# A two-layer gated cross-attention kernel: last output weights in the query weights' buffers, and new orders at the transitions

## The chip, the cores and the metric

One NeuronCore of one Trainium2 chip runs the whole computation in one launch. The metric is the device time of that launch in microseconds (us). Five engines run side by side, each through its own queue of instructions in a fixed order: TensorE (PE in the profile), VectorE (DVE), ScalarE (ACT), GpSimd (POOL) and SyncE (SP, which here only issues DMA transfers). They meet through semaphores: an instruction waits until a count is reached, and whatever stands behind it in its queue waits too.

## The reference

x is 16 sequences of 64 tokens with 512 features, 1024 tokens in all. Four blocks are each added to x through a gate.

```python
x = x + tanh(g_xattn[0]) * attention0(layernorm(x), ctx, mask0, rotary positions)   # 32 query heads, 8 key heads, D = 128
x = x + tanh(g_ffn[0])   * experts(layernorm(x))       # 16 experts of 56, top 2: silu(x g) * (x u), weighted, then d
x = x + tanh(g_xattn[1]) * attention1(layernorm(x), ctx, mask1)                     # RMS norm of queries and keys, no rotation
x = x + tanh(g_ffn[1])   * lora(layernorm(x))          # 4 low-rank experts of rank 16, top 2, softmax gates
```

Attention is softmax(q k / sqrt(D)) v, then the output weights.

## The kernel before

Every fp32 product on TensorE is made of three: each operand is split into a high part (a rounded copy that ScalarE writes, names in _hi) and a low part (the difference, names in _lo, by VectorE or GpSimd), and `three` (L213 to L217) issues hi*hi, hi*lo and lo*hi. So each weight that is loaded (_raw) needs a pass of ScalarE and one of GpSimd before TensorE can use it.

The stages in order: keys and values of both layers (`kv_*`, eight blocks, the last of them, LATE, runs inside the first attention step), attention of layer 0 (`att_*`, lay = 0), the experts (`moe_*`), attention of layer 1 (lay = 1), the low-rank experts (`lora_*`).

Attention has 8 groups g of J = 4 heads, and each is done for two halves h of the tokens: a unit u = 2g + h, from 0 to 15. The work is a software pipeline. `step(g, h)` projects the queries of unit u, makes scores and softmax of u - 1, and values and output projection of u - 2. Per unit the chain is: scores (PE, L867), transposition (`turn_scores`, DVE), for layer 1 a scale by the norms (`scale_scores`, from `square_sums`, `turn_sums` and `norms`), mask, `maxima` (a reduction and four 32x32 operations, L1214), `att_shift`, `exponentials` (ACT), `sums` (again with four small operations, and a reciprocal), `att_normalise`, `turn_probs`, `probs_high` (ACT), `att_probs_low`, then `values` (PE, L888), `out_high` (ACT), `out_low` (DVE), `project_out` (PE, L215 to L217 into ps_b) and `add_output` (DVE). In layer 0 a query is also rotated: `rotate` on DVE reads the bank in three operations, `rotate` on POOL (L1094) adds the two halves.

The order of every engine's queue is written out by hand, in one `step` for each engine (`att_act`, `att_pool`, `att_dve`, `att_pe`, `att_sync`). Steps at the ends have orders of their own: `first_scores` (layer 0, g = 0, h = 1), `second_first_scores` (the same in layer 1), `before_closing` (g = 7, h = 1), and what stands behind the loop, here called the closing: units 14 and 15 with nothing left to project. The first steps, to (1, 0), are called the opening.

In the closing the splits of the next stage's weights run beside: `beside(h, t)` calls `moe_beside_act` (ACT's high parts, by the table SPLITS) or `lora_beside_*`. The list `splits` counts router r, gate g, up u and down d pieces from 0 to 21, and GpSimd makes the low parts in the same order (`moe_pool`). The output weights of group g are split by `wo_high` (L977) and `wo_low` (L1087), those of the last group behind the last step, into the same wo_hi and wo_lo as all others. `ln_stat`, `ln_sd`, `ln_rs`, `ln_norm`, `ln_turn`, `ln_high` and `ln_low` are the steps of the layer norm. `tokens` in `moe_*` copies the normalised tokens of one tile to f_hi and f_lo, from which `up` reads.

On SP the spill of the LATE block stands ahead of the first loads of layer 0:

```python
kv_sync_spill(sp, LATE)                            # 8 transfers of 512 KB
sp.wait_ge(kv["v_spilled"], 16 * 2 * GB * 2 * NB)
...
load_wo(0)
load_v(0)
```

## Time and profile before

| | us |
|---|---|
| median of three runs | 1278.47 (1278.26 to 1282.9) |
| the profiled execution | 1278.5 |
| its span, first to last instruction | 1276.5 |
| TensorE busy | 1208.3 |
| mean granted clock of TensorE, share of full | 0.982 |

PE, PEld, DVE, ACT, POOL and SP are the engines; L977 is line 977 of the kernel. A timeline line gives the start and length in us, the engine, the line, the operation, output and inputs, shape and count, and in brackets how long the engine stood idle before it and which instruction released it. The busy share is an average over stages; an engine that is idle beside a busy TensorE costs nothing.

### The profile page before, as it was taken

What the parts mean: (1) busy time and instruction counts of PE and PEld (TensorE: products, weight loads), DVE (VectorE), ACT (ScalarE), POOL (GpSimd) and SP (SyncE); (2) the same over time, 40 slices, a digit from 0 to 9 for tenths busy, and PEclk for the clock granted to TensorE, in tenths of its full rate; (3) what the DMA queues carried; (4) which work ended last, traced back from release to release, by engine and by line L of the source; (5) the groups of instructions that cost most, each with busy time, mean ns of one, the idle gap of its engine ahead of it and who ended that gap; (6) DMA issues with size and microseconds to landing.
All of it is one profiled execution on the core that took longest, in us unless ns stands there. A gap on an engine that the chain in (4) does not pass through costs nothing.

```text
span 1276.5 us, 16865 instructions
## 1 busy us (share of the span) xinstructions
PE 1208.3 (95%) x6160; PEld 956.9 (75%) x6160; DVE 852.1 (67%) x1477; ACT 428.4 (34%) x732; POOL 581.9 (46%) x399
## 2 busy tenths in 40 slices
PE   7999999799999999999799999799999999999976
PEld 6887878587777877777588887577777777777664
DVE  4656635988888878888953125857666666757586
ACT  5144151222222222222353225444334344443422
POOL 4431432556767667574443112345455464544400
PEclk9999999899999999999799999999999999999997
DMA  7853730922212122212010003202122112211001
GB/s 264 265 149 123 240 118 22 301 79 74 74 53 101 43 74 74 82 42 99 1 59 33 1 0 130 82 9 101 48 74 74 49 66 82 74 41 42 33 1 67
DMA packets 57248, 106.73 MB, mean 84 GB/s; under 512 B 3504, under 2 KB 36272, under 8 KB 51824
## 3 DMA queue, kind: packets, MB, share of 16 engines
q1 hardware_dynamic: 56672, 105.04, 24.0%
q0 software_dynamic: 384, 1.05, 0.2%
q8 instruction: 30, 0.49, 0.2%
q14 instruction: 18, 0.15, 0.0%
q10 hardware_dynamic: 144, 0.00, 0.0%
HBM read 78.81 MB, written 27.26 MB: 83 GB/s over the span
## 4 chain that ended last, share of the span: by engine, by line
PE 67%; DVE 14%; POOL 8%; issue 6%; ACT 3%; DMA 1%; SPq 1%; POOLq 0%; ACTq 0%; DVEq 0%
PE ps_b L215 11%; PE ps_b L217 11%; PE ps_b L216 11%; PE ps_q L215 9%; PE ps_q L216 9%; PE ps_q L217 9%; DVE r_s L1198 2%; PE ps_s L867 2%; PE ps_b L888 2%; POOL qT L1094 2%; POOL wo_lo L1087 2%; PE ps_q L854 1%; DVE o_lo L1241 1%; POOL wq_lo L682 1%; DVE mx_c L1214 1%
## 5 line engine op out<-in xcount | busy, mean ns | idle before, releaser
L215 PE MATMUL ps_b<-wo_hi,o_hi 128*128 128x512 f32 x512 | 203.7, 398 | 12.9 <-DVE o_lo L1241 4.1
L215 PE MATMUL ps_q<-hT_hi,wq_hi 128*128 128x512 f32 x512 | 207.5, 405 | 5.7 <-ACT qT L986 4.4
L217 PE MATMUL ps_b<-wo_hi,o_lo 128*128 128x512 f32 x512 | 202.0, 394 | 0.0
L216 PE MATMUL ps_b<-wo_lo,o_hi 128*128 128x512 f32 x512 | 201.9, 394 | 0.0
L216 PE MATMUL ps_q<-hT_lo,wq_hi 128*128 128x512 f32 x512 | 200.3, 391 | 0.0
L217 PE MATMUL ps_q<-hT_hi,wq_lo 128*128 128x512 f32 x512 | 199.8, 390 | 0.0
L1241 DVE TENSOR_TENSOR o_lo<-ps_b,o_hi 128x512 fp32r<-128x512 f32 x128 | 82.4, 685 | 77.2 <-ACT o_hi L1011 75.8
L1250 DVE SCALAR_TENSOR_TENSOR x_sb<-ps_b,gates,x_sb 128x512 f32<-128x512 f32 x128 | 92.3, 727 | 61.4 <-PE ps_b L217 60.9
L1094 POOL TENSOR_TENSOR qT<-q_t 128x512 f32<-128x512 f32 x64 | 88.8, 1387 | 96.3 <-DVE q_t L1178 96.3
L215 PEld LDWEIGHTS ps_q<-hT_hi,wq_hi 128*128 128x128 f32 x512 | 96.3, 188 | 42.6 <-issue 15.2
L215 PEld LDWEIGHTS ps_b<-wo_hi,o_hi 128*128 128x128 f32 x512 | 97.9, 191 | 38.2 <-issue 13.8
L682 POOL TENSOR_TENSOR wq_lo<-wq_raw,wq_hi 128x512 fp32r<-128x512 f32 x64 | 89.5, 1403 | 55.1 <-ACT wq_hi L676 55.1
L217 PEld LDWEIGHTS ps_b<-wo_hi,o_lo 128*128 128x128 f32 x512 | 97.7, 191 | 20.9
L216 PEld LDWEIGHTS ps_b<-wo_lo,o_hi 128*128 128x128 f32 x512 | 97.8, 191 | 20.0
L217 PEld LDWEIGHTS ps_q<-hT_hi,wq_lo 128*128 128x128 f32 x512 | 96.4, 188 | 21.0
L216 PEld LDWEIGHTS ps_q<-hT_lo,wq_hi 128*128 128x128 f32 x512 | 96.5, 188 | 17.8
L1006 ACT ACTIVATE p_hi<-pT 128x1024 fp32r<-128x1024 f32 x32 | 33.9, 1060 | 204.1 <-DVE pT L1235 204.1
L1087 POOL TENSOR_TENSOR wo_lo<-wo_raw,wo_hi 128x512 fp32r<-128x512 f32 x64 | 85.7, 1356 | 28.7 <-ACT wo_hi L977 28.7
L735 POOL TENSOR_TENSOR p_lo<-pT,p_hi 128x1024 fp32r<-128x1024 f32 x27 | 64.2, 2380 | 63.1 <-ACT p_hi L1006 63.1
L1011 ACT ACTIVATE o_hi<-ps_b 128x512 fp32r<-128x512 f32 x128 | 66.4, 607 | 66.5 <-PE ps_b L888 66.4
L724 POOL TENSOR_TENSOR s_sb<-s_sb,mx_c 128x1024 f32<-128x1024 f32 x28 | 53.7, 1918 | 70.7 <-DVE mx_c L1214 70.7
L730 POOL TENSOR_TENSOR p_sb<-p_sb,p_rec 128x1024 f32<-128x1024 f32 x28 | 53.7, 1919 | 65.6 <-DVE p_rec L1229 65.6
(236 smaller groups left out, 2395.5 us busy)
## 6 DMA issues: line engine op xcount, KB each, us to landing
wq_raw<-in_wq SPq DMA_DIRECT2D x16, 1024.0 KB, 4.8
wo_raw<-in_wo SPq DMA_DIRECT2D x16, 1024.0 KB, 4.9
v_hi_spill<-vs_hi SPq DMA_DIRECT2D x16, 512.0 KB, 5.7
v_lo_spill<-vs_lo SPq DMA_DIRECT2D x16, 512.0 KB, 6.7
kT<-kT_spill SPq DMA_DIRECT2D x32, 256.0 KB, 4.3
v_hi<-v_hi_spill SPq DMA_DIRECT2D x16, 512.0 KB, 3.7
v_lo<-v_lo_spill SPq DMA_DIRECT2D x16, 512.0 KB, 4.6
kw_raw<-in_wk SPq DMA_DIRECT2D x4, 1024.0 KB, 8.9
```

Source lines behind the costliest of these rows:

```text
L215: nc.tensor.matmul(dst, l_hi, r_hi, start=first, stop=False)
L216: nc.tensor.matmul(dst, l_hi, r_lo, start=False, stop=False)
L217: return nc.tensor.matmul(dst, l_lo, r_hi, start=False, stop=last)
L682: nc.gpsimd.tensor_tensor(wq_lo[:, :, j * D:(j + 1) * D], wq_raw[:, :, j * D:(j + 1) * D], wq_hi[:, :, j * D:(j + 1) * D].bitcast(F32), AL ...
L724: eng.tensor_tensor(sc, sc, wide(mx_c[:, :], QB), ALU.subtract).then_inc(c["s_shifted"], 1)
L730: eng.tensor_tensor(pr, pr, wide(p_rec[:, :], QB), ALU.mult).then_inc(c["p_normed"], 1)
L735: eng.tensor_tensor(p_lo[:, :], pT[:, :], p_hi[:, :].bitcast(F32), ALU.subtract).then_inc(c["p_lo"], 1)
L1011: nc.scalar.activation(o_hi[:, 2 * half:2 * half + 2, :, par * S:(par + 1) * S], ps_b[n].rearrange("p (t j q) -> p t j q", t=2, j=J), ACT. ...
L1087: nc.gpsimd.tensor_tensor(wo_lo[:, j, :], wo_raw[:, j, :], wo_hi[:, j, :].bitcast(F32), ALU.subtract).then_inc(c["wo_lo"], 1)
L1094: nc.gpsimd.tensor_tensor(qT[:, h, j, :], q_t1[:, j % 2, :], q_t2[:, j % 2, :], ALU.add).then_inc(c["q_rot"], 1)
L1241: nc.vector.tensor_tensor(o_lo[part], ps_b[n].rearrange("p (t j q) -> p t j q", t=2, j=J), o_hi[part].bitcast(F32), ALU.subtract).then_inc ...
L1250: nc.vector.scalar_tensor_tensor(x_sb[:, i, :], ps_b[t][:, :], gates[:, lay:lay + 1], x_sb[:, i, :], ALU.mult, ALU.add).then_inc(c["y_adde ...
```

## The change

In words:

- The output weights of the last group go into wq_hi and wq_lo (`wo_parts`), whose last reader is the last query projection. So `wo_high` and `wo_low` of that group move into the step ahead of the closing, in both layers. `before_closing` holds for layer 1 too.
- GpSimd waits at the end of attention for the last p_lo; the expert splits come behind it, in the order r, g0 to g3, u0 to u3, g4 to g6, u4 to u6, d, and `up` waits for the pieces of its half. u_raw and d_raw lie elsewhere, the u load waits for the output projections of 14 units, the d load for all.
- The first three tiles of `up` read hT_hi and hT_lo directly, without `tokens`.
- Opening of layer 0: the LATE values are spilled in three parts (24 transfers), `load_v(0)` goes ahead of the last part, `load_wo(0)` behind it; shift and normalisation of unit 0 go from DVE to POOL; the maxima come ahead of the last value tile, and one more rotation is taken ahead.
- Opening of layer 1: `wo_high(0)` and `wo_low(0)` go one step earlier, the fourth query ahead of the exponential, and the next unit's `turn_sums` ahead of `sums`.
- Last closing: the mask goes from POOL to DVE, aT_lo and the clears from DVE to POOL, bT_lo to a later place; the order of layer 0 holds for both. The square root and reciprocal of the last layer norm become Ln and Exp on ScalarE.

```diff
...
-                                                    ("rT_lo", [P, KC, P], FR), ("gu1", [P, 2, FH], F32))
-        with ExitStack() as a:
-            d_raw, = alloc(a, ("d_raw", [P, FT, E], F32))
+            r_raw, rT_hi, rT_lo, gu1, d_raw = alloc(a, ("r_raw", [P, KC, P], F32), ("rT_hi", [P, KC, P], FR), ("rT_lo", [P, KC, P], FR),
+                                                    ("gu1", [P, 2, FH], F32), ("d_raw", [P, FT, E], F32))
...
 
+        with ExitStack() as a:
...
 
+        def ln_rs_act(act, c, h, parts=HALVES):
+            act.wait_ge(*c("moments", parts[h][1]))
+            own = slice(*parts[h])
+            nc.scalar.activation(ln_sd_sb[:, own], ln_mv[:, own, 1], ACT.Ln, bias=eps_ln[:, 0:1]).then_inc(c["sd"], 1)
+            act.wait_ge(*c("sd", h + 1))
...
+            v = VALUE_BLOCKS.index(LATE)
+            i0, i1 = part
+            sp.wait_ge(c["v_hi"], NT * v + i1)
+            sp.wait_ge(c["v_lo"], NT * v + i1)
+            for st, dr in ((vs_hi, v_hi_dram), (vs_lo, v_lo_dram)):
+                for g in range(GB):
+                    sp.dma_start(dr[lay, cb * GB + g, :, i0 * D:i1 * D].rearrange("p (i d) -> p i d", d=D),
+                                 st[:, i0:i1, g * D:(g + 1) * D].bitcast(F32)).then_inc(c["v_late"], 16)
...
-            return lay == 0 and isinstance(g, int) and (g, h) == (G - 1, 1)
+            return isinstance(g, int) and (g, h) == (G - 1, 1)
...
-                kv_sync_spill(sp, LATE)
-                sp.wait_ge(kv["v_spilled"], 16 * 2 * GB * 2 * NB)
+                kv_sync_late(sp, LATE_PARTS[0])
+                kv_sync_late(sp, LATE_PARTS[1])
+                sp.wait_ge(kv["v_spilled"], 16 * 2 * GB * LATE_VALUES)
+                sp.wait_ge(kv["tile"], NT * len(BLOCKS))
+                load_v(0)
+                kv_sync_late(sp, LATE_PARTS[2])
+                sp.wait_ge(kv["v_late"], LATE_SPILLS)
...
-            load_v(0)
...
+            return (wq_hi, wq_lo) if isinstance(g, int) and g == G - 1 else (wo_hi, wo_lo)
...
+                if isinstance(g, int) and g == G - 1:
+                    act.wait_ge(*c("q_done", J * 2 * G))
+                elif not (isinstance(g, int) and g == 0):
                     act.wait_ge(*c("y_done", 8 * g))
...
-                    if second_first_scores(lay, g, h):
-                        wo_high(0, j)
...
-                    if second_first_scores(lay, g, h) and j == 3:
-                        exponentials(us)
                     if do_project and lay:
-                        queries(uq, h, j)
+                        if not (isinstance(g, int) and (g, h, j) == (1, 0, 0)):
+                            queries(uq, h, j)
+                        if isinstance(g, int) and (g, h) == (0, 0):
+                            wo_high(0, j)
...
-                if do_score and not second_first_scores(lay, g, h):
+                if before_closing(lay, g, h):
+                    for j in range(J):
+                        wo_high(G - 1, j)
+                if do_score:
                     exponentials(us)
                 if next_wq:
                     att_wq_high(act, lay, g + 1, 3)
+                if first_scores(lay, g, h):
+                    wo_high(0, 0)
+                    wo_high(0, 1)
+                if second_first_scores(lay, g, h):
+                    queries(uq + 1, 0, 0)
                 if do_score:
                     probs_high(us)
                 if last_step(lay, g, h):
                     norms(us + 1)
                 if first_scores(lay, g, h):
-                    for j in range(J):
-                        wo_high(0, j)
+                    wo_high(0, 2)
+                    wo_high(0, 3)
...
-            for j in range(J):
-                wo_high(G - 1, j)
-            if lay:
-                beside(0, -1)
             for n in range(4):
                 out_high(last - 1, n)
-            if lay == 0:
-                beside(0, -1)
+            beside(0, -1)
             exponentials(last)
-            beside(0, 0)
             probs_high(last)
             if lay == 0:
                 nc.scalar.preload_act_table_set("sqrt_and_others")
             for n in range(4):
                 out_high(last, n)
-            ln_sd(act, lns[2 * lay + 1], 0)
+            beside(1, -1)
+            if lay:
+                ln_rs_act(act, lns[3], 0)
+            else:
+                ln_sd(act, lns[1], 0)
...
+                    att_shift(pool, lay, us)
                     split((), (0,))
                     added(2)
+                    added(3)
                     split((), (1,))
-                    added(3)
+                    att_normalise(pool, lay, us)
                     split((), (2, 3))
                     return
                 if second_first_scores(lay, g, h):
                     for j in range(J):
+                        att_wq_low(pool, lay, 1, j)
+                    return
+                if lay and isinstance(g, int) and (g, h) == (0, 0):
+                    for j in range(J):
                         wo_low(0, j)
-                        att_wq_low(pool, lay, 1, j)
                     return
...
                     att_shift(pool, lay, us)
+                if before_closing(lay, g, h):
+                    wo_low(G - 1, 0)
+                    wo_low(G - 1, 1)
                 added(3)
+                if before_closing(lay, g, h):
+                    wo_low(G - 1, 2)
...
             att_steps(pool, step)
-            for j in range(J):
-                wo_low(G - 1, j)
+            pool.wait_ge(*c("p_lo", 2 * G))
             if lay:
...
                     rotated(0)
                     rotated(1)
                     turn_scores(us, 1 - h)
+                    maxima(us)
                     kv_values_lo(dve, LATE, NT - 1)
                     rotated(2)
-                    maxima(us)
                     rotated(3)
-                    att_shift(dve, lay, us)
+                    sums(us)
                     rotate(uq + 1, 0, 0)
-                    sums(us)
-                    att_normalise(dve, lay, us)
                     turn_probs(us)
+                    rotate(uq + 1, 0, 1)
                     att_probs_low(dve, lay, us)
...
                         scale_scores(us)
...
+                att_mask(dve, lay, last, 1)
...
-            if lay:
-                out_low(last - 1, 2)
-                out_low(last - 1, 3)
             att_shift(dve, lay, last)
-            if lay:
-                add_output(last - 1, 0, 0)
...
+            out_low(last - 1, 2)
+            out_low(last - 1, 3)
+            sums(last)
+            att_normalise(dve, lay, last)
+            add_output(last - 1, 0, 0)
+            turn_probs(last)
+            for t in range(1, PAIRS):
+                add_output(last - 1, 0, t)
+            att_probs_low(dve, lay, last)
+            ln_stat(dve, ln, 0, added)
+            ln_stat(dve, ln, 1, added)
...
-            ln_rs(dve, ln, 0)
+            if lay == 0:
+                ln_rs(dve, ln, 0)
...
             sp.wait_ge(c["w_hi"], len(splits))
             sp.wait_ge(c["w_lo"], len(splits))
             sp.wait_ge(c["logits"], 2)
+            sp.wait_ge(c["hid"], 4)
             att_load_wq(sp, 1, 0)
 
 
 
-        splits = [("r", 0)] + [(w, n) for w in "gud" for n in range(FT)]
-        SPLITS = {(0, -1): (0, 1, 2, 3, 4, 5), (0, 0): (6, 7), (1, 0): (8,), (1, 1): (9, 10), (1, 2): (11, 12), (1, 3): (13, 14)}
+        splits = ([("r", 0)] + [(w, n) for w in "gu" for n in range(4)] + [(w, n) for w in "gu" for n in range(4, FT)]
+                  + [("d", n) for n in range(FT)])
+        GU_SPLITS = {("g", 0): 5, ("u", 0): 9, ("g", 1): 12, ("u", 1): 15}
...
 
@@ -1482,14 +1522,19 @@
 
             def up(i, r, half, between=None):
 
-                if half == 0:
-                    pe.wait_ge(c["f_hi"], i + 1)
-                    pe.wait_ge(c["f_lo"], i + 1)
+                direct = isinstance(i, int) and i < 3
+                if half == 0 and not direct:
+                    pe.wait_ge(c["f_hi"], i - 2)
+                    pe.wait_ge(c["f_lo"], i - 2)
                 if not (isinstance(i, int) and i == 0):
                     pe.wait_ge(c["gu"], 2 * i + half - 1)
                 for bank, hi, lo, name in ((ps_q[half], gT_hi, gT_lo, "g_done"), (ps_b[half], uT_hi, uT_lo, "u_done")):
+                    if isinstance(i, int) and i == 0:
+                        pe.wait_ge(c["w_lo"], GU_SPLITS[name[0], half])
                     for k in range(KC):
-                        last = three(bank[:, 0:FH], f_hi[:, r, k, :], f_lo[:, r, k, :], hi[:, k, half * FH:(half + 1) * FH],
...
             pe.wait_ge(*att[0]("y_added", 2 * G * PAIRS))
-            pe.wait_ge(c["w_lo"], 1 + 2 * FT)
...
@@ -1600,11 +1644,9 @@
                 hidden_hi(i - 1)
                 silu(i, 1)
 
-            act.wait_ge(c["w_lo"], 1 + FT)
-            tokens(0, 0)
             ln_sd(act, lns[1], 1)
             logits(0)
-            tokens(1, 1)
+            act.wait_ge(c["w_lo"], GU_SPLITS["g", 1])
             silu(0, 0)
...
@@ -1670,13 +1711,9 @@
                 weigh(i, 1)
 
             pool.wait_ge(*lns[1]("lo", PAIRS))
-            pool.wait_ge(c["w_lo"], 1 + FT)
-            tokens(0, 0)
-            tokens(1, 1)
+            pool.wait_ge(c["w_lo"], GU_SPLITS["g", 1])
             for n in range(FT):
                 split_low(pool, 1 + 2 * FT + n)
-                if n == 1:
-                    tokens(2, 0)
             pool.wait_ge(c["x_w"], 1)
...
-                ln_sd(nc.scalar, lns[3], 1, PARTS)
+                ln_rs_act(nc.scalar, lns[3], 1, PARTS)
...
+            if (h, t) == (1, 1):
                 nc.vector.wait_ge(lora["w_hi"], 2)
                 nc.vector.scalar_tensor_tensor(bT_lo[:, :], b_raw[:, :], LORA_SCALE, bT_hi[:, :].bitcast(F32), ALU.mult,
                                                ALU.subtract).then_inc(lora["w_lo"], 1)
+
+        def lora_pool(pool):
+            pool.wait_ge(*att[1]("q_done", J * 2 * G))
...
             ln_norm(dve, lns[3], NT - 2)
-            ln_rs(dve, lns[3], 2, PARTS)
...
```

## Rows read from the trace of the kernel before

**Rows 1.** Page: busy time and share of each engine; 40 slices
```profile
PE 1208.3 (95%) x6160; PEld 956.9 (75%) x6160; DVE 852.1 (67%) x1477; ACT 428.4 (34%) x732; POOL 581.9 (46%) x399
...
PE   7999999799999999999799999799999999999976
...
PEclk9999999899999999999799999999999999999997
```

**Rows 2.** Waits of TensorE: total us, times, longest us
```profile
PE ps_q L854 <- ACT q_sq L985: 5.2, 2, 4.5
PE ps_b L888 <- DVE x_sb L1250: 4.7, 1, 4.7
...
PE ps_s L867 <- POOL qT L1094: 4.4, 1, 4.4
PE ps_b L888 <- DMA v_lo<-v_lo_spill: 3.6, 1, 3.6
```

**Rows 3.** Timelines, opening of layer 0: start us, length us, what, idle before
```profile
234.34 2.27 PE L867 MATMUL ps_s<-qT,kT 128*64 128x256 f32 x10 [4.40 <-POOL qT L1094]
...
253.62 0.47 PE L215 MATMUL ps_b<-wo_hi,o_hi 128*128 128x512 f32 x1 [0.20 <-POOL wo_lo L1087]
...
231.98 2.31 POOL L1094 TENSOR_TENSOR qT<-q_t 128x512 f32<-128x512 f32 x1 [2.69 <-DVE q_t L1178]
...
242.47 1.23 DVE L735 TENSOR_TENSOR p_lo<-pT,p_hi 128x1024 fp32r<-128x1024 f32 x1 [1.12 <-ACT p_hi L1006]
...
227.52 7.24 SPq L407 DMA_DIRECT2D v_lo_spill<-vs_lo  x4
239.59 0.34 SPq L741 DMA_DIRECT2D wo_raw<-in_wo  x1
...
240.45 0.43 SPq L748 DMA_DIRECT2D v_lo<-v_lo_spill  x1
```

**Rows 4.** Windows of 2 us, TensorE: stretch, length, busy, clock, DMA, GB/s
```profile
608.00:610.00 2.00, 0.00 (x0) 1.00 0.00 0
610.00:612.00 2.00, 1.89 (x5) 0.50 0.00 0
...
614.00:616.00 2.00, 2.00 (x10) 1.00 0.00 0
```

**Rows 5.** Timelines, closing of layer 0
```profile
592.49 0.77 DVE L1214 TENSOR_TENSOR mx_c<-mx_a 32x32 f32<-32x32 f32 x4
...
606.54 2.28 DVE L718 TENSOR_TENSOR s_sb<-s_sb,mask_i 128x1024 f32<-128x1024 f32 x1
...
611.18 5.03 DVE L1214 TENSOR_TENSOR mx_c<-mx_a 32x32 f32<-32x32 f32 x4
616.24 2.25 DVE L724 TENSOR_TENSOR s_sb<-s_sb,mx_c 128x1024 f32<-128x1024 f32 x1
...
619.71 1.22 DVE L1225 TENSOR_REDUCE sm_a<-p_sb 128x32 f32<-128x1024 f32 x1
...
612.39 7.23 POOL L1449 TENSOR_TENSOR gT_lo<-g_raw,gT_hi 128x512 fp32r<-128x512 f32 x5
...
629.88 0.39 PE L888 MATMUL ps_b<-p_hi,v_hi 64*128 64x256 f32 x2 [2.73 <-DVE p_lo L735]
```

**Rows 6.** Timelines, opening of the expert layer
```profile
644.77 7.53 POOL L1449 TENSOR_TENSOR uT_lo<-u_raw,uT_hi 128x512 fp32r<-128x512 f32 x6 [3.28 <-ACT uT_hi L1444]
...
653.28 0.44 PE L215 MATMUL ps_q<-gT_hi,f_hi 128*128 128x448 f32 x1 [1.56 <-POOL f_lo L1655]
...
647.11 0.70 DVE L223 BATCH_NORM_STATS2 ln_stats<-x_sb 128x6 f32<-128x512 f32 x1
```

**Rows 7.** Timelines, opening of layer 1
```profile
818.37 1.93 PE L854 MATMUL ps_q<-q_sq,ones 128*32 128x512 f32 x8 [4.52 <-ACT q_sq L985]
...
816.68 1.15 ACT L999 ACTIVATE p_sb<-s_sb,zero_b 128x1024 f32<-128x1024 f32 x1 [3.30 <-DVE s_sb L724]
...
809.48 4.92 DVE L1214 TENSOR_TENSOR mx_c<-mx_a 32x32 f32<-32x32 f32 x4
...
825.05 1.23 DVE L735 TENSOR_TENSOR p_lo<-pT,p_hi 128x1024 fp32r<-128x1024 f32 x1 [1.13 <-ACT p_hi L1006]
```

**Rows 8.** Timelines, closing of layer 1
```profile
1206.09 5.97 POOL L1087 TENSOR_TENSOR wo_lo<-wo_raw,wo_hi 128x512 fp32r<-128x512 f32 x4
1212.03 2.37 POOL L718 TENSOR_TENSOR s_sb<-s_sb,mask_sb 128x1024 f32<-128x1024 f32 x1
...
1228.31 0.58 PE L888 MATMUL ps_b<-p_hi,v_hi 64*128 64x256 f32 x2 [4.67 <-DVE x_sb L1250]
```

88 lines of the change are left out of this document (38 added, 50 removed).

## The prediction

> **What bounds the kernel now.** I read the busy shares and the 40 slices first. TensorE is busy 95% of the span, and the clock row is at 9 (its top digit) but for one 8 and two 7s, in slices where the work changes kind [rows 1]. Inside the long attention loops there is nothing to win: TensorE is full, and the other engines have room. Everything lies in some 68 us where TensorE isn't busy (1276.5 less 1208.3), and in the stretches where its clock is low because it had just waited. TensorE's list of waits names the places [rows 2]: 5.2 us for squares from ScalarE, 4.7 for an added output, 4.4 for a rotated query, 3.6 for the values' load. By their times they belong to the four transitions of attention: the two openings (about 225 to 254 and 788 to 838) and the two closings (605 to 653 and 1203 to 1236). The kernel's first 20 us and its last 25 us also have gaps, and the change leaves nearly all of those alone.
>
> **The clock.** After the 2.97 us gap ahead of 610.12 the granted clock is 0.50, that is 1.2 GHz, and from 614 it is 1.00 (2.4 GHz) again [rows 4]. 24 matmuls take 7.3 us there and 5.6 us at full clock, so a gap that long costs 1.7 us more than its own length. A gap that shrinks enough gives that back too; a gap that only moves doesn't.
>
> **Opening of layer 0.** Now TensorE stands 4.40 us until 234.34, for the rotated query that GpSimd makes at 231.98 with a stretched 2.31 us [rows 3]. It is late because VectorE takes the score maxima ahead of the last rotation. Then it stands 3.6 us for the values, queued on SP behind eight spills of 512 KB (the last four issue over 7.24 us) and the output weights. After: the spill goes in parts as tiles are ready, and values load right after the last tile. GpSimd takes shift and normalisation, VectorE has them no more and reaches the last rotation some 2.5 us sooner; score(1) can start near 230.6, a gain of 3.7, plus 1.6 of clock, since the gap left is under 1 us. From there I walk each queue with the durations of before. VectorE: sums and rotation to 234.9, transposition of probabilities to 236.2, the second rotation to 238.3, low halves of probabilities to 239.5, or 240.6 if GpSimd's output-weight splits hold it up; values(0) start there and not at 247.2. But what comes next is late: the fourth wo_lo stands in GpSimd's queue behind the third query's addition, and that waits for VectorE's mask and rotation (about 246). So wo_lo ends near 248.6 and the first output projection starts at 248.7, against 253.62 now [rows 3]. That is 4.9 us, less 1.7, since the new 4 us gap ahead of it brings a low clock: **-3.3**. The load of the output weights now waits for the last small spills. I cost those at 0.4 us an issue (the values' issues on the same queue take 0.43): 224.5 to 228, landed by 231, weights there by 236 and their splits just ahead of p_hi, which ScalarE's order puts behind two of them. By the nearest spill rows, 7.24/4 = 1.81 us each, it would be 14.5 us for eight, and the weights would land near 250 and hold p_hi up: +5. Ends: -6 to +5. I take the small price because each piece is an eighth of the size of those in [rows 3].
>
> **Rule against it.** The Trainium skill (DMA: Bandwidth & Descriptors, Measured) says that transfers under 64 KB are dominated by descriptors and wants 1 MiB; the change cuts 8 transfers into 24, the last eight of 64 KB. By its 0.95 us for 64 KB the last eight would be an estimated 7.6 us and the weights about 4 us later than I say, so that the term would be 0 to +1.
>
> **Closing of layer 0.** The chain is VectorE's. While GpSimd works without a pause through wo_lo, router and gate splits (five of them in 7.23 us), four 32x32 maxima take 5.03 us; ten microseconds earlier, with GpSimd idle, the same four take 0.77 [rows 5]. The shift takes 2.25 for 1.23, the mask 2.28 for 1.23, the sums 2.27 for 0.77: together 7.8 us over. The change sets these splits aside until after the last p_lo, and makes the four wo_lo a step earlier, in the query weights' buffers, whose last reader ends at 592.4. Not free: they now stand ahead of the normalisation in GpSimd's queue, and the four small sums of that step (0.77 us at 598.56) will be held up three times. Normalisation ends near 604.5 and not 601.7, the low halves at 608.2 and not 605.35, so values(14) start **2.75 us later**. From 608.2: transposition, mask, two low outputs, maxima, shift, two low outputs, exponential, sums, normalisation come to 620.3; probabilities turned by 622.3. Now TensorE is late next: its four projections start at 612.2, take 11.2 us at full clock, 12.2 with half a low stretch, and the last addition and p_lo follow: 626.4. Values(15) start at 629.88 now [rows 5]: **-3.5**, ends -6 (clock up, chain of VectorE alone) and 0 (clock low through both pairs).
>
> **Opening of the expert layer.** TensorE waits 1.56 us for f_lo until 653.28, after the last of the u splits [rows 6]. The change reads hT directly and waits only for the splits of its half: -1.56. Against it: the splits now run from p_lo on, beside the layer norm, so that the first two normalisations (SBUF to SBUF, 0.50 each) each wait up to 1.3 us, and ln_sd stands behind four u_hi (2.5 us, covered by the first projection at low clock, 4.9 us now). **-1.3**, ends -1.6 and 0. The u load moves to the end of projection 13 (603) and needs some 8 to 10 us; its first reader is at 629. The d load is covered as well.
>
> **Opening of layer 1.** TensorE stands 4.52 us until 818.37 for q_sq, which is queued on ScalarE behind the exponential (816.68, itself waiting for VectorE's shift, whose four maxima took 4.92 us beside GpSimd) [rows 7]. After: squares come first, the wo splits are in the step before. That step pays 0.7 us (two ln_high later by 0.6, a normalisation beside wo_lo). Then: TensorE free at 814.6, squares at 815.2, sums and score to 818.2, projections to 820.9, 823.7, 826.5. VectorE blocks on turn_sums until 816.3, then copies (some held up by the last wq_lo) to 819.6, sums to 821.9, normalisation, transposition, and p_lo to 826.9, against 826.28 now [rows 7]. So values(0) start at 827.0 instead of 833.20, and nothing of 1.27, 0.26 and the low clock is left. The fourth projection ends at 831.4 and o_lo is there: **-6.3** against 837.67. Ends -7.5 and -4: p_lo has 0.5 us to spare at most, and each microsecond it is late costs one.
>
> **Closing of layer 1.** Here the four wo_lo (5.97 us) hold the mask on GpSimd until 1214.40 [rows 8]. After: wo_lo a step earlier, mask and p_lo on VectorE. The price is as in layer 0: the exponential 0.9 later, sums and normalisation 2.1 later, values(14) at 1207.1 for 1206.23. Scale, mask and low outputs then run to 1212.2; TensorE starts its projections there and not at 1209.76, after a 3.4 us gap, so at low clock: 1225.1 for the fourth, p_lo 1227.1, values(15) at 1227.15 for 1228.31. **-1.5** with 0.3 for a shorter stay at the low clock; ends -4.5 (no low clock) and +1.5. Ln and Exp on ScalarE for a square root and VectorE's reciprocal put some 0.15 us on each of two late steps: **+0.3**, ends 0 and +0.6.
>
> **Sum.** -3.3 - 3.5 - 1.3 - 6.3 - 1.5 + 0.3 = -15.6. The profiled execution took 1278.5 (span 1276.5 and 2.0 around it), the median of three is 1278.47: 1262.9.
>
> **Rivals.**
> - *Only the openings pay* (0.17). In both closings the 2.75 and 0.9 us at the front and the clock eat the rest. For: the chain there hops engines at each step, and TensorE's last projections are next in line. Against: 7.8 us of hold-ups go. 1278.5 - 3.3 - 1.3 - 6.3 + 0.3 = 1267.9.
> - *The clock stays up* (0.14). If the gaps that are left no longer pull it down in three of the stretches I costed low, 3 x 1.7 more: 1257.8. For: a gap of 1.27 in the opening of layer 1 didn't. Against: the one of 2.46 ahead of 619.84 did.
> - *The late spill isn't cheaper* (0.07), that is, the opening of layer 0 doesn't become what the change says: +5 for -3.3: 1271.2. It decides once the output weights land after about 237.
> - *GpSimd's splits hold up the layer norm* (0.05), the slower case. All fifteen expert splits now run between p_lo(15) and the end of the router's product. If each held up one instruction on VectorE's chain, 15 x 1.26 = 18.9: 1281.8. Against: bn_stats took 0.70 us amid six u splits (7.53 us) [rows 6], and so did PSUM readers; only the normalisations were stretched. It becomes slower from about twelve holds on. The Trainium skill (SBUF — State Buffer, Who interferes with whom) has the same rule: an instruction with two SBUF inputs, or tensor_scalar in a two-port mode, is fully blocked by GpSimd, tensor_reduce and a single SBUF input are not. The trace agrees (sm_a 1.22 us beside a split, 1.22 alone).
> - The rest, 0.57, is the forecast.
>
> **How the numbers follow.** The likeliest case gives 1263. The range 1254 to 1271 takes in the clock case and the openings-only case and most of the terms' ends, which don't all fall together. A change of 0.5% is 6.4 us, about what a measurement of this kernel can tell from none. Below 1272.1: forecast, openings only, clock, and a part of the spill case, 0.90; above 1284.9: 0.03, the far end of the split case; between: 0.07.
>
> **What would show it.** Right: no wait for q_sq near 814 and values(0) of layer 1 about 13 us after it; mx_c x4 near 0.8 us in both closings, and sm_c of the step before at 2.5 or more; up(0) right behind the router's product; p_lo of layer 0 near 240, with a wait for wo_lo after it. Wrong: wo_raw landing after 237, the first projection of layer 0 after 250, values(15) of the closings no earlier than now, a layer norm longer than now by over 2 us.

## Result and profile after

The changed kernel takes **1263.32 us** (median of 4 runs, 1261.83 to 1264.48), the kernel before, beside it, 1279.14 us. The ratio is 0.9872, 95% interval 0.9852 to 0.9893. The forecast was 1263. The profiled execution took 1262.69 us, of which 1260.7 are its span.

The page of the changed kernel, busy time and slices:

```profile
PE 1204.3 (96%) x6160; PEld 955.8 (76%) x6160; DVE 840.5 (67%) x1471; ACT 425.3 (34%) x730; POOL 577.9 (46%) x399
...
PEclk9999999999999999999899999999999999999987
```

Against [rows 1], TensorE does the same 6160 matmuls with 4.0 us less of busy time (part of it is the clock: 0.984 on average for 0.982), and of the digits 8 and 7 in mid span only one is left. VectorE is busy 11.6 us less: part of that are its hold-ups by GpSimd, part is work that changed engines. TensorE's list of waits (total us, times, longest) shows what took the places of [rows 2]:

```profile
PE ps_b L921 <- DVE p_lo L759: 8.7, 4, 2.7
...
PE ps_b L215 <- POOL wo_lo L1125: 6.4, 7, 3.7
```

The four waits of 4.7 to 3.6 us are gone from the list: square sums and rotated query wait 0.69 and 0.64 us at most. In their place are four shorter waits for low halves of probabilities (2.71, 2.02, 1.93 and 2.02 us), one of 3.25 us ahead of the projections in the closing of layer 1, and one new one of 3.70 us, which is the one that the prediction names: the fourth wo_lo of the opening of layer 0. The opening of layer 0, timelines of the changed kernel (start us, length us, what, idle before):

```profile
223.60 1.80 SPq L430 DMA_DIRECT2D v_hi_spill<-vs_hi  x4
225.44 1.85 SPq L430 DMA_DIRECT2D v_lo_spill<-vs_lo  x4
229.06 0.33 SPq L765 DMA_DIRECT2D wo_raw<-in_wo  x1
...
233.86 1.15 ACT L1009 ACTIVATE wo_hi<-wo_raw 128x512 fp32r<-128x512 f32 x2 [6.91 <-DMA wo_raw<-in_wo]
...
229.80 1.51 PE L900 MATMUL ps_s<-qT,kT 128*64 128x256 f32 x12 [0.64 <-POOL qT L1132]
...
238.76 0.39 PE L921 MATMUL ps_b<-p_hi,v_hi 64*128 64x256 f32 x2 [0.60 <-issue]
...
247.11 0.77 PE L215 MATMUL ps_b<-wo_hi,o_hi 128*128 128x512 f32 x1 [3.70 <-POOL wo_lo L1125]
```

The last eight pieces take 3.65 us on SP's queue, 0.45 us each, where [rows 3] has 1.81. Score(1) starts at 229.80 for 234.34, values(0) at 238.76 for 247.23, the first projection at 247.11 for 253.62. Then the clock, in windows of 2 us (stretch, length, busy of PE, PEld, DVE, ACT and POOL, clock, DMA share, GB/s):

```profile
249.00:251.00 2.00, 2.00 (x6) 1.63 (x5) 1.90 (x3) 1.15 (x1) 0.59 (x1) 0.50 1.04 434
...
253.00:255.00 2.00, 2.00 (x10) 1.64 (x10) 1.94 (x5) 0.00 (x0) 0.00 (x0) 0.98 0.00 0
```

Behind the 3.70 us wait TensorE runs at 1.2 GHz until some 253; the 48 matmuls of the first projection take 2.8 us longer than in the kernel before (the first of the next group starts 13.78 us after 247.11, and 10.98 us after 253.62 before).

The closing of layer 0, VectorE and TensorE:

```profile
594.81 3.19 DVE L1262 TENSOR_TENSOR sm_c<-sm_a 32x32 f32<-32x32 f32 x4
...
608.80 0.77 DVE L1262 TENSOR_TENSOR mx_c<-mx_a 32x32 f32<-32x32 f32 x4
609.61 1.23 DVE L748 TENSOR_TENSOR s_sb<-s_sb,mx_c 128x1024 f32<-128x1024 f32 x1
...
604.12 0.39 PE L921 MATMUL ps_b<-p_hi,v_hi 64*128 64x256 f32 x2 [2.71 <-DVE p_lo L759]
...
622.64 0.39 PE L921 MATMUL ps_b<-p_hi,v_hi 64*128 64x256 f32 x2 [2.02 <-DVE p_lo L759]
```

The maxima, 5.03 us in [rows 5], take 0.77, the shift 1.23 for 2.25. The price is in the first line: the sums of the step before take 3.19 us for 0.77. In the opening of the expert layer, up(0) starts at 643.44 right behind the router's product, without the wait of 1.56 us of [rows 6]. The opening of layer 1:

```profile
806.71 1.06 PE L887 MATMUL ps_q<-q_sq,ones 128*32 128x512 f32 x8 [0.69 <-ACT q_sq L1017]
818.52 0.39 PE L921 MATMUL ps_b<-p_hi,v_hi 64*128 64x256 f32 x2 [0.49 <-issue]
...
800.88 0.77 DVE L1262 TENSOR_TENSOR mx_c<-mx_a 32x32 f32<-32x32 f32 x4
```

0.69 us of waiting where [rows 7] has 4.52, and values(0) 11.8 us after it.

### The profile page after: what moved, and what is told of

Same layout as the page of the kernel before. It is cut to its first block, busy times and chain, and to the rows that moved or that the text cites. A ratio compares the mean times of both kernels' runs of the same rounds, so it can differ in the third digit from the quotient of the medians.

```text
span 1260.7 us, 16869 instructions
## 1 busy us (share of the span) xinstructions
PE 1204.3 (96%) x6160; PEld 955.8 (76%) x6160; DVE 840.5 (67%) x1471; ACT 425.3 (34%) x730; POOL 577.9 (46%) x399
## 4 chain that ended last, share of the span: by engine, by line
PE 72%; DVE 11%; POOL 7%; issue 6%; ACT 3%; DMA 0%; POOLq 0%; ACTq 0%; DVEq 0%
PE ps_b L215 12%; PE ps_b L217 12%; PE ps_b L216 12%; PE ps_q L215 10%; PE ps_q L216 9%; PE ps_q L217 9%; PE ps_s L900 3%; PE ps_b L921 3%; DVE r_s L1246 2%; POOL qT L1132 2%; POOL wo_lo L1125 2%; POOL wq_lo L706 1%; PE ps_q L887 1%; POOL p_sb L754 1%; DVE o_lo L1289 1%
## 5 line engine op out<-in xcount | busy, mean ns | idle before, releaser
L215 PE MATMUL ps_b<-wo_hi,o_hi 128*128 128x512 f32 x448 | 176.2, 393 | 6.4 <-POOL wo_lo L1125 6.4
L216 PE MATMUL ps_b<-wo_lo,o_hi 128*128 128x512 f32 x448 | 175.5, 392 | 0.0
L217 PE MATMUL ps_b<-wo_hi,o_lo 128*128 128x512 f32 x448 | 175.3, 391 | 0.0
L215 PEld LDWEIGHTS ps_b<-wo_hi,o_hi 128*128 128x128 f32 x448 | 84.8, 189 | 27.5 <-issue 10.0
L217 PEld LDWEIGHTS ps_b<-wo_hi,o_lo 128*128 128x128 f32 x448 | 84.8, 189 | 17.8
L216 PEld LDWEIGHTS ps_b<-wo_lo,o_hi 128*128 128x128 f32 x448 | 84.8, 189 | 17.5
L1125 POOL TENSOR_TENSOR wo_lo<-wo_raw,wo_hi 128x512 fp32r<-128x512 f32 x56 | 73.5, 1327 | 13.2 <-ACT wo_hi L1009 13.2
```

Source lines behind the costliest of these rows:

```text
L215: nc.tensor.matmul(dst, l_hi, r_hi, start=first, stop=False)
L216: nc.tensor.matmul(dst, l_hi, r_lo, start=False, stop=False)
L217: return nc.tensor.matmul(dst, l_lo, r_hi, start=False, stop=last)
L1125: nc.gpsimd.tensor_tensor(lo[:, j, :], wo_raw[:, j, :], hi[:, j, :].bitcast(F32), ALU.subtract).then_inc(c["wo_lo"], 1)
```

## Experiments

All are edits of one of the two kernels. Ratios are to the kernel before, timed on the same chip beside them; where I give a difference to the changed kernel "by the ratios", it is the difference of two ratios times the kernel before. In the traces I compare distances between two instructions of the same execution, so that a gain elsewhere doesn't mix in. S(n), V(n) are score(n) and values(n).

**1. The opening of layer 1 alone.** The kernel before with the new order of layer 1's opening: squares and wo splits a step earlier, the exponential in its place of the step, the sums of rows turned behind it, wo_lo on GpSimd in the first step.

```
 ACT  second step of layer 1
-    wo_high(0, j)           # now in the first step
-    if j == 3: exponentials(us)
     queries(uq, h, j)
 ...
+exponentials(us)
 ...
+queries(uq + 1, 0, 0)       # first query of the next step
```

> The kernel before with the new opening of layer 1 alone (wo splits of group 0 one step earlier, fourth query ahead of the exponential, turn_sums of the next unit ahead of the sums). Theory: the transitions are independent terms, and this one is worth 6.3 us by itself: values(0) of layer 1 start 6.3 us sooner after the last expert product, and the time is 6.3 us (0.5%) under the kernel before. Rival: the stretch was only short because the stages ahead of it had moved too; then it gives under 3 us.

Measured: 1272.1 us (1269.85 to 1273.14), ratio 0.9951 (0.9937 to 0.9964). From the first square sums of layer 1 to the first out projection it is 31.03 us, as in the changed kernel (37.87 before). The other transitions take what they took before, to 0.1 us; what differs is the time before the late tile (0.9 us less) and behind values(15) of layer 1 (2.1 us more, with more of it at the low clock), where this edit changes nothing. TensorE in this kernel:

```profile
813.96 1.07 PE L854 MATMUL ps_q<-q_sq,ones 128*32 128x512 f32 x8 [0.69 <-ACT q_sq L985]
825.78 0.39 PE L888 MATMUL ps_b<-p_hi,v_hi 64*128 64x256 f32 x2 [0.49 <-issue]
```

From the last expert product to values(0) it is 6.36 us less than before. So this part alone is worth what its term says (-6.3), and it doesn't need the others.

**2. Which of the moves in that opening counts.** The changed kernel with the exponential ahead of the fourth query's squares again.

```
 for j in range(J):
+    if second_first_scores(lay, g, h) and j == 3:
+        exponentials(us)
     queries(uq, h, j)
 ...
-if do_score:
+if do_score and not second_first_scores(lay, g, h):
     exponentials(us)
```

> The changed kernel, but in the opening of layer 1 ScalarE takes the exponential ahead of the fourth query again, as before the change. Theory: the 4.52 us came from the late shift (four maxima held up for 4.92 us by GpSimd's splits), not from the place of the exponential; with the splits gone the shift ends at 802.9, before the fourth query is projected at 806.0, so this costs nothing: the wait ahead of the square sums stays 0.7 us and the time within 0.5 us of the changed kernel. Rival: the place in ScalarE's queue is the cause; then 2 to 4.5 us of the wait come back.

Measured: 1259.84 us, ratio 0.9853 (0.9838 to 0.9868), 2.4 us under the changed kernel by the ratios, with intervals that overlap. The wait ahead of the square sums is the same 0.69 us:

```profile
808.53 1.07 PE L887 MATMUL ps_q<-q_sq,ones 128*32 128x512 f32 x8 [0.69 <-ACT q_sq L1017]
```

What had held the squares up was the late exponential (VectorE's maxima amid GpSimd's splits), and the splits in ScalarE's queue, not the order of exponential and squares; how much each of the two counts isn't separated. This order is even 0.55 us better to the first out projection (30.48).

**3. The hold of the expert splits.** The changed kernel without GpSimd's wait for the last p_lo in layer 0, so that the splits run during the closing as they did before.

```
-pool.wait_ge(*c("p_lo", 2 * G))
 if lay:
+    pool.wait_ge(*c("p_lo", 2 * G))
     lora_pool(pool)
```

> The changed kernel, but GpSimd doesn't wait for the last p_lo in layer 0, so that router and first gate splits run beside the chain of VectorE again. Theory (GpSimd blocks VectorE's instructions with two SBUF inputs): mx_c x4 in the closing goes from 0.77 to about 5 us, p_lo(15) comes 3 to 4 us later (1.8 us of VectorE's slack before it are used up first), and the time is 2 to 4.5 us above the changed kernel. Rival: the closing is bound by TensorE's projections and hand-overs between engines; then values(15) start within 1 us of the changed kernel's.

Measured: 1265.39 us, ratio 0.9908 (0.9893 to 0.9923). VectorE and GpSimd:

```profile
608.37 4.48 DVE L1262 TENSOR_TENSOR mx_c<-mx_a 32x32 f32<-32x32 f32 x4
612.89 2.25 DVE L748 TENSOR_TENSOR s_sb<-s_sb,mx_c 128x1024 f32<-128x1024 f32 x1
...
609.03 5.02 POOL L1489 TENSOR_TENSOR gT_lo<-g_raw,gT_hi 128x512 fp32r<-128x512 f32 x4
```

The hold-up is back with the splits, same place, same instructions: 4.48 us for 0.77. From S(15) to V(15) it is 25.98 us, with the splits held 23.18 and 21.45 in the two profiled executions of the changed kernel. By the ratios the kernel is 4.6 us above the changed one, at the upper end of what I expected (its one profiled execution, 1262.96 us, is no longer than the changed kernel's, since the clock stayed up in two later places). The mechanism of the term for this closing is shown. The Trainium skill (SBUF — State Buffer, Who interferes with whom) has a VectorE instruction with two SBUF inputs wait for a GpSimd instruction that reads SBUF and was issued first. This pair of traces agrees and adds that one of 32x32 is hit as hard as one of 128x1024: the four lose 3.71 us, 0.93 each, the shift loses 1.02, and one split lasts 1.26.

**4. The old order of SP's queue.** The changed kernel with the whole late spill, and the values behind the output weights, as before.

```
-kv_sync_late(sp, LATE_PARTS[0])
-kv_sync_late(sp, LATE_PARTS[1])
-...
-load_v(0)
-kv_sync_late(sp, LATE_PARTS[2])
+kv_sync_spill(sp, LATE)
 load_wo(0)
+load_v(0)
```

> The changed kernel with the old order on SyncE: the whole late spill after the last tile, then output weights, then values. All other orders stay. Theory: the three-part spill carries the opening of layer 0: with the old one wo_raw lands near 243.5 and not 233.8, p_hi waits behind two wo_high, values(0) start about 8 us later, the first projection of the output 4 to 6 us later, and the time is 4 to 6 us above the changed kernel. Rival: the orders of VectorE and GpSimd carry it (the last rotation 3 us sooner); then the time is within 2 us of the changed kernel.

Measured: 1271.07 us, ratio 0.9952 (0.9937 to 0.9968): 10.2 us over the changed kernel by the ratios, twice what I had expected.

```profile
227.56 7.25 SPq L415 DMA_DIRECT2D v_lo_spill<-vs_lo  x4
239.65 0.34 SPq L765 DMA_DIRECT2D wo_raw<-in_wo  x1
...
248.97 0.58 PE L916 MATMUL ps_b<-p_hi,v_hi 64*128 64x256 f32 x2 [11.17 <-DVE p_lo L759]
```

The gap grows to 11.17 us, since in the new order of ScalarE the high half of the probabilities stands behind two wo_hi, and they wait for the weights. From the last matmul of the late tile to the first projection it is 37.1 us; 26.7 in the changed kernel, 32.2 before. Of these 10.4 us the group of 48 behind it gives some back, since it runs at full clock here (10.98 us, for 13.78 and 12.58 in the changed kernel): 7.6 to 8.8 us are left in the trace, and the rest of the 10.2 isn't placed. **Without the new spill the rest of this opening would lose 5 us.** It isn't a sum of two gains: one edit makes the other possible. Experiments 9 and 10 part the two halves of the spill's change.

**5. wo_lo ahead of the additions.** The prediction put the late fourth wo_lo down to its place in GpSimd's queue, behind an addition. Here the four wo_lo stand together, and VectorE makes the third rotation ahead of the maxima and behind the low outputs.

```
 added(0)
-wo_low(0, 0)
-wo_low(0, 1)
+for j in range(J): wo_low(0, j)
 added(1)
-wo_low(0, 2)
 added(2)
-wo_low(0, 3)
```

> The changed kernel with two moves in the opening of layer 0: GpSimd makes all four low parts of the first output weights ahead of the second rotated query, and VectorE takes the first two low outputs ahead of the third rotation. Theory (what is late next there is the fourth wo_lo, which stands behind a rotation in two queues): the 3.70 us wait ahead of the first output projection falls to 1 to 1.7 us, TensorE's clock then stays up and gives back some 2.8 us more, and the time is 4 to 5 us under the changed kernel. Rival: the wait only moves, to the low outputs or to values(1); then under 2 us.

Measured: 1258.34 us (1252.03 to 1261.39), ratio 0.9836 (0.9811 to 0.9860), beside 0.9866 for the changed kernel on the same chip (8, below): 3.8 us by the ratios and 2.7 by the medians, with intervals that overlap; I had given 4 to 5. The trace is clearer. GpSimd, then TensorE:

```profile
239.06 6.98 POOL L1125 TENSOR_TENSOR wo_lo<-wo_raw,wo_hi 128x512 fp32r<-128x512 f32 x4
...
246.18 0.47 PE L215 MATMUL ps_b<-wo_hi,o_hi 128*128 128x512 f32 x1 [1.25 <-POOL wo_lo L1125]
```

The wait is 1.25 us for 3.71, the projection starts 24.27 us after the late tile for 26.71, and the clock stays up: the windows over 246 to 254 read 1.00, and the group of 48 takes 10.99 us, where the changed kernel took 13.78 and 12.58. That is 2.4 plus 1.6 to 2.8: 4.0 to 5.2 us in the trace.

**6. Two wo splits on either side of the normalisation.** In the steps before both closings, GpSimd makes two of the wo_lo behind the normalisation, to take away the price that the first lines of the closing show (3.19 us of sums).

```
-if before_closing(lay, g, h):
-    wo_low(G - 1, 2)
-    wo_low(G - 1, 3)
 split((), (2,))
 if do_score:
     att_normalise(pool, lay, us)
+if before_closing(lay, g, h):
+    wo_low(G - 1, 2)
+    wo_low(G - 1, 3)
```

> The changed kernel, but in the step ahead of both closings GpSimd makes two of the four wo_lo ahead of the normalisation and two behind it. Theory (three of the four small sums wait for GpSimd's splits): sm_c x4 goes from 3.2 us to about 1.3 in layer 0 and from 2.2 to about 1 in layer 1, and values(14) start 1.5 to 2 us sooner in layer 0 and 1 us sooner in layer 1; since values(15) hang on the same chain, the time falls by 1.5 to 3 us. Rival: values(15) are bound by TensorE's four projections after values(14) and its clock; then what is won ahead is lost there and the time stays within 1 us.

Measured: 1260.84 us, ratio 0.9873 (0.9858 to 0.9888): no difference that can be measured from the changed kernel (0.9866), and none of the 1.5 to 3 us that my theory gave. In layer 0 the edit does what it should:

```profile
593.89 1.10 DVE L1262 TENSOR_TENSOR sm_c<-sm_a 32x32 f32<-32x32 f32 x4
...
601.10 0.39 PE L921 MATMUL ps_b<-p_hi,v_hi 64*128 64x256 f32 x2 [0.62 <-issue]
604.72 0.47 PE L215 MATMUL ps_b<-wq_hi,o_hi 128*128 128x512 f32 x1 [1.92 <-ACT o_hi L1043]
```

V(14) start 2.56 us after S(15) for 4.66, and the wait of 2.71 is gone; but the gap before the projections is 1.92 now and the clock goes down behind it (0.79 in 605 to 613), so that S(15) to V(15) is 20.96 us, for 23.18 and 21.45 in the two profiled executions of the changed kernel. In layer 1 it loses 0.7 us. The sums there are down to 0.77 us, but the moved splits now lie beside the copies of the row sums, 4.09 us for 2.07:

```profile
1178.99 0.77 DVE L1262 TENSOR_TENSOR sm_c<-sm_a 32x32 f32<-32x32 f32 x4
...
1181.48 4.09 DVE L1246 COPY r_s<-r_t 32x16 f32<-32x16 f32 x8
...
1182.10 2.53 POOL L1125 TENSOR_TENSOR wq_lo<-wo_raw,wq_hi 128x512 fp32r<-128x512 f32 x2
```

I had left that neighbour out. My theory held in layer 0 for values(14) and fell in layer 1. The time is where the rival put it (within 1 us), and the low clock that it named was seen, but with intervals of some 2 us on either side the times don't decide it.

**7. All three moves** (2, 5 and 6) in one kernel.

> The two kernels before this one together, and the exponential first in layer 1 (0.5 us sooner in its trace). Theory: the terms add up, 6 to 8.5 us under the changed kernel, about 1254 to 1256, ratio to the kernel before about 0.981. Rival: the gains overlap in a clock that falls by chance in the closings, and less than 4 us are left.

Measured: **1254.62 us** (1251.49 to 1256.99, 5 runs), ratio 0.9818 (0.9800 to 0.9837), the fastest of all: 1.8% under the kernel before, and 6.5 us under the changed kernel, with intervals that don't overlap: what I expected (6 to 8.5), and not the rival's under 4. Windows of this kernel over the closing of layer 0:

```profile
602.00:610.00 8.00, 8.00 (x36) 6.58 (x36) 7.72 (x17) 2.45 (x4) 0.00 (x0) 1.00 0.00 0
```

The same gap of 1.9 us ahead of the projections as in 6, and here the clock stays at 2.4 GHz. Left as it was in layer 1, where it loses 0.7 us, the move of 6 might leave this kernel a little faster still; that wasn't tried.

**8. The changed kernel again**, on the chip of 5 to 7.

> The changed kernel once more, beside the others. Theory: 15 to 17 us under the kernel before. The stretch from the last expert product to the first query of layer 1 took 4.9 us in some traces and 6.5 us in others, behind the same wait of 1.94 us and the same instructions, by whether the clock fell; both lengths are expected again over the four traces of this call.

Measured: 1261.08 us (1258.32 to 1262.73), ratio 0.9866 (0.9849 to 0.9884). Its windows behind the same wait of 3.71 us:

```profile
249.00:251.00 2.00, 2.00 (x7) 1.58 (x6) 1.97 (x4) 0.05 (x1) 1.92 (x1) 0.58 0.74 213
...
253.00:255.00 2.00, 2.00 (x11) 1.64 (x10) 1.92 (x3) 0.00 (x0) 0.65 (x1) 1.00 0.19 68
```

The same gap costs 1.6 us of clock here and 2.8 in the first execution: how long TensorE stays at 1.2 GHz isn't settled by the gap. The second half of what I had expected missed: both lengths of the stretch at the end of the expert layer were to be seen in the four traces of 5 to 8, and all four show the long one, with the low clock.

**9. The values last, the pieces kept.**

```
-load_v(0)
 kv_sync_late(sp, LATE_PARTS[2])
 sp.wait_ge(kv["v_late"], LATE_SPILLS)
+load_v(0)
```

> The changed kernel, but in the opening of layer 0 SP loads the first values behind the small late spills and their landing, ahead of the output weights, and no longer ahead of the last eight pieces; the pieces stay. It separates the two halves of the change to SP's queue: cutting the spills, and moving the values. Mine (the pieces carry it): the two value loads took 0.8 us on the queue, the small spills are issued about 1.3 us sooner, the values are issued near 227.5 instead of 221 and land by 233, the output weights are issued some 0.9 us later (their wait for the pieces counts from 226), and nobody reads the values before 238.8: values(0) and the first output projection start within 0.7 us of the changed kernel's, and the time is that of the changed kernel, ratio 0.985 to 0.989. Rival (the early values carry it): the values land behind the weights and hold up values(0) as in the kernel before, 3 us or more, ratio 0.990 or more.

Measured: 1263.38 us, ratio 0.9885 (0.9863 to 0.9907). By the ratio it is my case, but by the trace neither theory's: V(0) starts 2.7 us later after S(1), not under 0.7.

```profile
229.18 0.32 SPq L771 DMA_DIRECT2D v_hi<-v_hi_spill  x1
...
230.01 0.43 SPq L765 DMA_DIRECT2D wo_raw<-in_wo  x1
...
237.31 1.15 ACT L1009 ACTIVATE wo_hi<-wo_raw 128x512 fp32r<-128x512 f32 x2 [10.15 <-DMA wo_raw<-in_wo]
...
241.70 0.39 PE L921 MATMUL ps_b<-p_hi,v_hi 64*128 64x256 f32 x2 [3.37 <-issue]
```

The weights are issued 0.95 us later than in the changed kernel, as I had said, but the first wo_hi starts 7.30 us after the issue instead of 4.80: 1 MB of values is on its way just ahead of 1 MB of weights, and that is what this edit changes on the queue. What is late is the load behind them: ScalarE's high half of the probabilities stands behind two wo_hi, and V(0) behind it. Loading them early is worth 2.5 us to the first projection (26.7 for some 29.2), through the weights.

**10. The spill whole, the values ahead of it.**

```
-LATE_PARTS = ((0, 4), (4, NT - 1), (NT - 1, NT))
+LATE_PARTS = ((0, NT),)
...
 load_v(0)
-kv_sync_late(sp, LATE_PARTS[2])
+kv_sync_late(sp, LATE_PARTS[0])
```

> The changed kernel, but the late value block is spilled in eight issues of 512 KB, all after the last tile, as in the kernel before, and only the values' load ahead of them, as in the changed kernel. Mine (the pieces carry it): the values are there early, but the eight issues still take some 11.5 us from about 222 and the output weights wait some 4.8 us more for the landing: weights issued near 239, fourth high half near 245, and ScalarE's high half of the probabilities, which stands behind two of them, near 246; values(0) near 249 and the time that of the kernel with the old order throughout, ratio 0.994 to 0.997. Rival (the early values carry it): values(0) start near 239 to 241 and the ratio is 0.989 or less. The large step of that earlier kernel, 10.2 us where I had given 4 to 6, would be explained by mine: the wait for the weights on ScalarE delays values(0) by 10.2 us (238.76 to 248.97).

Measured: 1270.39 us, ratio 0.9931 (0.9915 to 0.9948). SP and TensorE:

```profile
226.19 4.24 SPq L430 DMA_DIRECT2D v_hi_spill<-vs_hi  x4
230.47 7.19 SPq L430 DMA_DIRECT2D v_lo_spill<-vs_lo  x4
242.59 0.34 SPq L765 DMA_DIRECT2D wo_raw<-in_wo  x1
...
251.75 0.58 PE L919 MATMUL ps_b<-p_hi,v_hi 64*128 64x256 f32 x2 [11.06 <-issue]
```

With the values in time, V(0) still start 19.4 us after S(1), as in experiment 4 (19.5), for 9.0 in the changed kernel. The ratio is a little under the 0.994 to 0.997 that I had given. The pieces carry the opening: eight whole issues take 11.5 us of the queue and 4.9 more to land, eight of 64 KB take 3.7 and 1.8.

## Why the prediction was right

The sum came out right (-15.6 forecast, -15.8 in the spans), with terms that are right in their mechanism and partly by luck in their size. Stages are measured between the same instructions of two executions, each against the profiled execution of the kernel before. The last column is the second profiled execution of the changed kernel (experiment 8), which ran as long as the first:

| step | forecast, us | found, us | found in 8, us |
|---|---|---|---|
| before the late tile | 0 | -1.0 | +0.3 |
| opening of layer 0 | -3.3 | -2.7 | -3.9 |
| closing of layer 0, to values(15) | -3.5 | -3.5 | -5.2 |
| layer norm, to the router | 0 | -0.9 | +0.3 |
| opening of the expert layer | -1.3 | -1.7 | -1.7 |
| end of the expert layer | 0 | +1.5 | +1.5 |
| opening of layer 1 | -6.3 | -6.3 | -6.3 |
| closing of layer 1, to values(15) | -1.5 | -1.5 | -1.5 |
| Ln/Exp and the end | +0.3 | +0.3 | +0.8 |

**Opening of layer 0.** The queue walk held: score(1) 229.80 (230.6 said), values(0) 238.76 (239.5 to 240.6), the projection 247.11 (248.7), and the new wait has the length that I gave (3.70 for 4). The place of the fourth wo_lo in GpSimd's queue is its cause, as experiment 5 shows. But nothing in that queue waits for VectorE there, as I had it: the third rotation ends at 244.19, and GpSimd works without a pause from 236.29 to 246.97.

```profile
241.02 2.27 POOL L1132 TENSOR_TENSOR qT<-q_t 128x512 f32<-128x512 f32 x1
...
244.48 1.27 POOL L1132 TENSOR_TENSOR qT<-q_t 128x512 f32<-128x512 f32 x1
245.70 1.27 POOL L1125 TENSOR_TENSOR wo_lo<-wo_raw,wo_hi 128x512 fp32r<-128x512 f32 x1
```

What makes the fourth wo_lo late are the two additions ahead of it, 3.5 us, the first of them stretched beside VectorE's mask. The times are 1.0 us early because the whole execution was so by then. 5.5 us are gained to the first projection (4.9 said; 4.9 less 1.7 is 3.2, and not the 3.3 of the sum). The mis-sized term is the **low clock** behind the new wait: 1.7 us from [rows 4], found 2.8 in one execution and 1.6 in the other. The small pieces took 0.45 us each for my 0.4. The Trainium skill (DMA: Bandwidth & Descriptors, Measured) has its 0.95 us for 64 KB from loads that GpSimd issues; the 7.6 us estimated from it for the eight are twice the 3.65 that these stores took on SP's queue, and more than the 5.5 to the issue of the weights: the trace decides. With 4 us more the term would have been near +1, and experiments 9 and 4 show that by then nearly each microsecond of the weights counts: the first wo_hi 3.2 and 11.1 us later put the projection 2.5 and 10.4 us later. The upper end, +5, was priced too low for its own condition, weights near 250: in experiment 4, where they are there at 244.6, the opening is already 4.8 us longer than before. And what experiment 4 was expected to cost (4 to 6) didn't fit the prediction's own numbers, by which -3.3 against +5 is 8.3, within the 7.6 to 8.8 of its trace.

**Closing of layer 0.** The price at the front was 2.4 us for my 2.75, the sums held for 2.4 us in all (3.19 for 0.77). The gain is the maxima and the shift, as said, and experiment 3 gives it back by letting the splits run. (The undisturbed maxima of [rows 5] lie 19 us ahead of the stretched ones, and not ten as I wrote. And the sm_a of 1.22 us that I took as beside a split is so for half of its length; mx_a at 609.94, 1.21 us wholly beside the wo_lo splits, bears it out better.) The low clock from 604 to 612 (0.58, 0.56) is in the forecast. That the term came out to the tenth is luck all the same: in the seven traces with this order of the closing and the splits held (the changed kernel's two, 2, 4, 5, 9 and 10) the gain is 2.4 to 5.4 us, by how long the clock is low between S(15) and V(15).

**Expert layer.** Up(0) right behind the router, -1.56 as said; the layer norm was no more than 0.3 us longer, so the split rival (0.05) had nothing for it. The 0.9 us by which it was shorter in the first execution are the clock, which stayed up behind values(15) there (1.00 from 611) and was low in the kernel before and in experiment 8. What I said of the first two normalisations holds: they took 2.13 us together, 1.00 before.

**Opening of layer 1.** -6.3 to the tenth, in one kernel with all and in one with this part alone. The reason I gave, that the squares are queued behind the exponential, was half of it: experiment 2 leaves that order and keeps the gain. What mattered is that the exponential is no longer late.

**Closing of layer 1.** Values(14) 0.8 later (0.9 said), values(15) 1.5 earlier than in [rows 8] against score(15), with a wait of 3.25 us and a low clock behind it, as said. In experiments 2 and 3 the clock stayed up behind the same wait, and the gain was 3.1 and 3.2 us.

**The end.** That Ln and Exp cost 0.3 us isn't shown: no run changes them alone, and from values(15) to the end kernels with the same end take 46.5 to 51.0 us, the kernel before 48.2 and, in experiment 1 with its end, 50.2.

**What cancelled.** The two terms that I didn't have, -1.0 at the start and +1.5 at the end of the expert layer, lie where nothing that was changed works on the path. The first is spread: over the twelve profiled executions the late tile ends at 220.0 to 223.0, and at 221.4 and 220.5 in two that are the same up to there (the kernel before and experiment 1). The second is the clock. Before and after, TensorE waits 1.94 us for the same operand; the first two lines are of the changed kernel, the third is of the kernel before, where that wait ends at 781.17:

```profile
771.24 0.50 PE L215 MATMUL ps_b<-dT_hi,hdT_hi 128*128 128x512 f32 x1 [1.94 <-DVE hdT_lo L1742]
...
772.00:774.00 2.00, 2.00 (x6) 1.51 (x6) 1.93 (x5) 1.73 (x2) 2.00 (x3) 0.50 0.07 27
...
782.00:784.00 2.00, 2.00 (x10) 1.66 (x9) 1.90 (x6) 1.67 (x2) 2.00 (x3) 1.00 0.57 231
```

Behind it the clock is 0.50 in the changed kernel and 1.00 in the kernel before and in experiments 1 and 3. All nine traces that hold the expert splits back show the low clock at this place, the three that don't hold them back show the full one. So this 1.5 us may belong to the change and not to chance; what would connect the two stays open, and the prediction had no term for it. The 0.2 us by which the forecast missed is therefore partly luck: terms of up to 1.7 us that it lacked or that vary with the clock cancelled, in the two executions in different places. The runs of one kernel spread by as much (2.6 us here, 4.4 in experiment 8).

**What no experiment takes apart.** The direct reads of `up`, the closing of layer 1 and, in the opening of layer 0, the shift and normalisation on GpSimd and the new place of the maxima are measured only in the whole. The terms for the opening of layer 1, the spill and the held splits are the ones that runs show by themselves.

## To carry to other kernels

Before a small operation is moved on VectorE's queue, list what GpSimd does beside it: its splits stretched four 32x32 operations from 0.77 to 5 us, and wherever they were moved they held up the next small ones (sums, then copies); hold them back until the chain is through. A load on the critical path is late through what is issued and in flight ahead of it, even if nobody waits for that: cut the last part of a large store, and put other loads before or behind, not beside. When an edit makes a new wait, count it twice, as its length and as the low clock behind it, and take that second part as a range.

## What the runs showed of the hardware

- A gap of the same length brings the clock down in one execution and not in another: 1.94 us before the last of the down projection (0.50 behind it in the changed kernel, 1.00 before), 1.9 us in the closing of layer 0 (0.79 over 8 us in experiment 6, 1.00 in 7), and also longer ones: 3.25 us in the closing of layer 1 (low in seven of nine traces, full in experiments 2 and 3), 3.37 us ahead of V(0) in experiment 9 (full). The eight gaps of 3.48 to 3.72 us in the opening of layer 0 all had the low clock behind them, with 1.6 to 2.8 us lost where I measured it. Those of 1.25 and 1.27 us in the same place (experiments 5 and 7) didn't; near the end of the kernel it goes down at a gap of 0.76 us.
- A store of 64 KB took 0.45 us of SP's queue, one of 192 KB 0.50 to 0.62, of 256 KB 0.57 to 0.90, of 512 KB 1.06 to 1.81. The rise isn't by size alone: the first four of the whole spill took 4.24 us and the next four 7.19 to 7.25. What makes the second four slower stays open.
